# Half of the head expansion on VectorE, narrower mask matmuls and new planner constants in a two-layer attention and expert kernel

## What is computed

```python
x = x + layernorm(attn(layernorm(x)))
x = x + layernorm(ffn(layernorm(x)))
# attn: x += global causal attention; x += local attention over a window of 32 tokens
#       16 query heads of 8, 4 key/value heads, rope, norm of each q and k head, softmax
# ffn:  a shared expert plus the one expert of 8 with the highest router probability,
#       weights quantised to -1, 0, 1 times a scale for each row
```

## Time and profile before

| | us |
|---|---|
| median of 3 runs | 707.4 |
| the profiled execution, its time | 709.0 |
| the profiled execution, its span | 707.3 |
| TensorE busy | 542.5 (77%) |
| VectorE busy | 404.9 (57%) |
| ScalarE busy | 354.2 (50%) |
| GpSimd busy | 234.5 (33%) |

### The profile page before, as it was taken

One profiled execution on the slowest core, in us unless ns is written; L12 is line 12 of the kernel. 1 busy time (PEld: TensorE's weight loads), 2 busy tenths in 40 slices (PEclk: granted clock), 3 DMA queues, 4 the chain that ended last, 5 costly groups with the idle time before them and its releaser, 6 DMA issues.

```text
span 707.3 us, 15690 instructions
## 1 busy us (share of the span) xinstructions
PE 542.5 (77%) x5734; PEld 268.9 (38%) x5749; DVE 404.9 (57%) x1054; ACT 354.2 (50%) x490; POOL 234.5 (33%) x624
## 2 busy tenths in 40 slices
PE   1226649868896989889988989889999999538354
PEld 1204225424453443544444454344335343434242
DVE  2663966455476575757665566545535642654665
ACT  1021326854663578447846765666696678004010
POOL 3524784275256226411560211401110331050100
PEclk9956568997998999999999999999999999679666
DMA  8000000000000000000000000000000000000000
GB/s 233 1 0 1 1 2 1 2 1 1 2 3 1 1 10 1 2 1 9 1 2 2 8 3 1 9 2 2 9 1 2 1 10 2 1 0 2 7 0 8
DMA packets 8809, 6.17 MB, mean 9 GB/s; under 512 B 1944, under 2 KB 8096, under 8 KB 8736
## 3 DMA queue, kind: packets, MB, share of 16 engines
q10 hardware_dynamic: 3424, 2.64, 1.3%
q1 hardware_dynamic: 5312, 2.52, 1.3%
HBM read 4.11 MB, written 1.05 MB: 7 GB/s over the span
## 4 chain that ended last, share of the span: by engine, by line
PE 42%; DVE 23%; POOL 18%; issue 10%; ACT 5%; DVEq 1%; SPq 0%; DMA 0%; POOLq 0%; ACTq 0%
PE osum_g L900 11%; PE scores L874 8%; PE misc L1008 5%; ACT prob L733 5%; PE misc L997 4%; PE scores L868 3%; PE misc L900 3%; POOL qe_l L657 2%; POOL ke_l L662 2%; DVE early L1319 2%; DVE qT L1213 2%; PE misc L850 1%; PE misc L936 1%; PE misc L841 1%; DVE early L1360 1%
## 5 line engine op out<-in xcount | busy, mean ns | idle before, releaser
L733 ACT ACTIVATE prob<-scores 128x1024 f32<-128x1024 f32 (+3 forms) x352 | 307.5, 931 | 177.0 <-PE scores L874 174.2
L900 PE MATMUL osum_g<-prob,V 128*32 128x256 f32 (+1 forms) x2304 | 173.8, 392 | 12.0 <-ACT oTs_g L742 4.4
L874 PE MATMUL scores<-qT,kT 64*128 64x512 bf16 (+3 forms) x760 | 128.2, 358 | 26.9 <-ACT prob L733 13.3
L673 POOL TENSOR_SCALAR_AFFINE_SELECT prob<-prob 128x512 f32<-128x512 f32 x64 | 40.9, 660 | 140.1 <-ACT prob L733 139.9
L874 PEld LDWEIGHTS scores<-qT,kT 64*128 64x128 bf16 x760 | 34.9, 93 | 136.2 <-issue 121.9
L900 PEld LDWEIGHTS osum_g<-prob,V 128*32 128x32 f32 x2304 | 52.4, 111 | 75.8 <-issue 56.7
L1008 PE MATMUL misc<-t2T,h1p 128*128 128x512 bf16 x177 | 46.2, 414 | 10.6 <-DVE h1p L1353 5.8
L690 POOL TENSOR_SCALAR frs<-fmv 128x1 f32<-128x1 f32 x16 | 3.7, 229 | 149.6 <-DVE fmv L1376 149.4
L997 PE MATMUL misc<-early,t1T 128*128 128x256 bf16 x384 | 47.5, 285 | 1.0 <-DVEq L1322 0.6
L1360 DVE TENSOR_TENSOR early<-misc,oh 128x512 f32<-128x512 f32 x32 | 22.0, 687 | 37.3 <-PE misc L1008 36.4
L997 PEld LDWEIGHTS misc<-early,t1T 128*128 128x128 bf16 x384 | 38.2, 102 | 10.4 <-issue 3.6
(11 more groups left out here) (210 smaller groups left out, 794.1 us busy)
## 6 DMA issues: line engine op xcount, KB each, us to landing
X<-in_L_attn_hidden_dram SPq DMA_DIRECT2D x8, 128.0 KB, 4.7
early<-in_L_ffn_expert_w_dram ACTq DMA_DIRECT2D x1, 1024.0 KB, 7.6
out_dram<-X SPq DMA_DIRECT2D x16, 64.0 KB, 1.5
rope<-in_rope_dram SPq DMA_DIRECT2D x1, 256.0 KB, 3.4
early<-in_L_ffn_shared_w_dram ACTq DMA_DIRECT2D x2, 128.0 KB, 8.0
wraw_l<-in_L_attn_l_wq_dram ACTq DMA_DIRECT2D x1, 64.0 KB, 2.5
ident<-in_ident_dram SPq DMA_DIRECT2D x1, 64.0 KB, 2.4
wraw_g<-in_L_attn_g_wq_dram SPq DMA_DIRECT2D x1, 64.0 KB
```

The costliest lines, as they stand in the source:

```text
L673: pool.affine_select(out=d, in_=d, compare_op=ALU.is_ge, fill=0.0, base=0, pattern=[[0, 4], [1, P]], channel_multiplier=-1).then_inc(mask_ ...
L733: act.activation(prob[:, n % NP, :, lo:hi], src, ACT.Exp, scale=float(HD) ** -0.5).then_inc(exp_done, 1)
L874: ins = pe.matmul(o[:, :, c:c + w], kT[a][rows, g, P * (t % kept[a]):P * (t % kept[a]) + P], qT[a][rows, b % Q_KEPT[a], 2 * g:2 * g + 2, q ...
L900: ins = pe.matmul(o[32 * m:32 * m + 32, q:q + w], V[a][:, t % kept[a], g, :], prob[:, n % NP, j, c:c + w], start=(first and k == 0), stop= ...
```

## The change

The second half (i = 1) of `expand` goes from GpSimd to VectorE in all 16 fronts; each mask matmul is cut into four of 32 columns; entries of `COST`, `HOP` and `PULL` are new, and while no global score unit is left to place (`blocks` empty), the chains `local`, `attend` and `norms` have 0.5 more pull (`LATE`). The kernel's steps are otherwise the same; their order is what the planner makes of the new numbers.

```diff
+SHARED = [(a, b, 1) for a in (G, L) for b in range(NB)]
...
-    "weights": [(PE, 9.016)], "prep": [(DVE, 13.229)], "ternary": [(DVE, 3.0)], "wturn": [(PE, 0.6), (DVE, 0.6)],
-    "scales": [(DVE, 2.221), (PE, 0.428), (DVE, 1.452)], "stat": [(DVE, 0.7), (POOL, 2.0)], "norm": [(DVE, 0.7)],
+    "weights": [(PE, 9.016)], "prep": [(DVE, 13.229)], "ternary": [(DVE, 3.343)], "wturn": [(PE, 0.6), (DVE, 0.6)],
+    "scales": [(DVE, 2.406), (PE, 0.26), (DVE, 2.02)], "stat": [(DVE, 0.7), (POOL, 2.0)], "norm": [(DVE, 0.7)],
...
-    "split": [(DVE, 2.209)], "expand": [(POOL, 2.134)], "kT": [(PE, 0.8), (DVE, 0.6)], "qT": [(PE, 0.55), (DVE, 0.7)],
+    "split": [(DVE, 2.461)], "expand": [(POOL, 2.134)], "kT": [(PE, 0.8), (DVE, 0.6)], "qT": [(PE, 0.55), (DVE, 0.7)],
...
-    "oevac": [(ACT_E, 0.3)], "pv": [(PE, 0.388)], "fstat": [(DVE, 1.169), (POOL, 0.662)],
+    "oevac": [(ACT_E, 0.3)], "pv": [(PE, 0.556)], "fstat": [(DVE, 1.169), (POOL, 0.662)],
...
-    "fw1": [(PE, 3.404)], "fz": [(DVE, 0.614)], "fact": [(ACT_E, 1.229)], "fh1": [(DVE, 3.219)], "fw2": [(PE, 5.916)],
-    "fsel": [(DVE, 2.299)], "fw2s": [(PE, 0.614)], "fsum": [(DVE, 1.218), (POOL, 1.433)], "fout": [(DVE, 0.884)],
+    "fw1": [(PE, 3.404)], "fz": [(DVE, 0.534)], "fact": [(ACT_E, 1.023)], "fh1": [(DVE, 2.39)], "fw2": [(PE, 5.916)],
+    "fsel": [(DVE, 2.299)], "fw2s": [(PE, 0.768)], "fsum": [(DVE, 1.218), (POOL, 1.433)], "fout": [(DVE, 1.017)],
 }
-HOP = 0.537
+HOP = 0.803
...
+LATE = {"close": 0.0, "local": 0.5, "attend": 0.5, "norms": 0.5, "feed": 0.0}
...
 PULL = {
-    "pv": -0.5, "close": 0.66, "local": 0.9, "attend": 0.931, "norms": 1.43, "feed": 0.0, "front": 0.5, "qk": 0.0,
-    "evac": 0.3,
+    "pv": -0.5, "close": 0.806, "local": 0.9, "attend": 0.169, "norms": 0.447, "feed": 0.0, "front": 0.5, "qk": 0.0,
+    "evac": -0.073,
 }
...
+    if s[0] == "expand" and s[1:] in SHARED:
+        return [(DVE, 1.8)]
     return COST[s[0]]
...
-                options.append((tried(s, c.start())[0] - PULL[c.name], c.name, c))
+                pull = PULL[c.name] + (0.0 if blocks else LATE.get(c.name, 0.0))
+                options.append((tried(s, c.start())[0] - pull, c.name, c))
...
             def expand(a, b, i):
 
+                if (a, b, i) in SHARED:
+                    return
                 pool.wait_ge(part_ready[a], b + 1)
...
-                        pe.matmul(o[:, :, lo:end], identb[:], bias.unsqueeze(1).broadcast_to([P, 2, end - lo]),
-                                  start=True, stop=False, skip_group_check=True)
+                        for k in range(4):
+                            pe.matmul(o[32 * k:32 * k + 32, :, lo:end], identb[:, 32 * k:32 * k + 32],
+                                      bias.unsqueeze(1).broadcast_to([P, 2, end - lo]), start=True, stop=False,
+                                      skip_group_check=True)
...
+            def expand(a, b, i):
+
+                if (a, b, i) not in SHARED:
+                    return
+                dve.wait_ge(part_ready[a], b + 1)
+                if b:
+                    dve.wait_ge(kT_ready[a], b)
+                    dve.wait_ge(qT_ready[a], 2 * b)
+                for p, (lo, n) in enumerate([(0, 3), (3, 3), (6, 2)]):
+                    src = part[a][:, p, i, 0:P].rearrange("p (h d) -> p h d", d=HD)
+                    dve.tensor_copy(qe[a][:, i, :, lo:lo + n, :], src.unsqueeze(2).broadcast_to([P, H, n, HD]))
+                for p in range(3):
+                    src = part[a][:, p, i, P:QKW].rearrange("p (h d) -> p h d", d=HD)
+                    n = 3 if p < 2 else 2
+                    ins = dve.tensor_copy(ke[a][:, i, :, p::3, :], src.unsqueeze(2).broadcast_to([P, KVH, n, HD]))
+                ins.then_inc(term_ready[a], 1)
```

More of the change, by code:

```diff
@@ L115 @@
     "fohT": [(PE, 0.223), (DVE, 1.031)], "fmask": [(PE, 0.647), (DVE, 2.0)], "fw1s": [(PE, 0.624), (DVE, 0.998)],
-    "fw1": [(PE, 3.404)], "fz": [(DVE, 0.614)], "fact": [(ACT_E, 1.229)], "fh1": [(DVE, 3.219)], "fw2": [(PE, 5.916)],
-    "fsel": [(DVE, 2.299)], "fw2s": [(PE, 0.614)], "fsum": [(DVE, 1.218), (POOL, 1.433)], "fout": [(DVE, 0.884)],
+    "fw1": [(PE, 3.404)], "fz": [(DVE, 0.534)], "fact": [(ACT_E, 1.023)], "fh1": [(DVE, 2.39)], "fw2": [(PE, 5.916)],
+    "fsel": [(DVE, 2.299)], "fw2s": [(PE, 0.768)], "fsum": [(DVE, 1.218), (POOL, 1.433)], "fout": [(DVE, 1.017)],
 }
-HOP = 0.537
+HOP = 0.803
 STALL_PE, STALL_OTHER = 0.98, 0.432
-KNOBS = {"fronts": 2, "feed": 30.371}
+LATE = {"close": 0.0, "local": 0.5, "attend": 0.5, "norms": 0.5, "feed": 0.0}
+KNOBS = {
+    "fronts": 2, "feed": 30.371,
+}
 PULL = {
-    "pv": -0.5, "close": 0.66, "local": 0.9, "attend": 0.931, "norms": 1.43, "feed": 0.0, "front": 0.5, "qk": 0.0,
-    "evac": 0.3,
+    "pv": -0.5, "close": 0.806, "local": 0.9, "attend": 0.169, "norms": 0.447, "feed": 0.0, "front": 0.5, "qk": 0.0,
+    "evac": -0.073,
 }
@@ L1383, in _ @@
             run = {"weights": weights, "prep": prep, "ternary": ternary, "wturn": wturn, "scales": scales,
-                   "stat": stat, "norm": norm, "proj": proj, "split": split, "kT": k_copy, "qT": q_copy,
+                   "stat": stat, "norm": norm, "proj": proj, "split": split, "expand": expand, "kT": k_copy, "qT": q_copy,
                    "oT": o_scale, "wo": residual, "fstat": fstat, "fxa": fxa, "fh": fh_norm,
```

## The result

Twenty runs of the changed kernel took 702.98 to 706.93 us, median 704.9. Twenty of the kernel before took 706.66 to 715.32 us, median 708.8. The ratio of the two is 0.9927, 95% interval 0.9906 to 0.9947. That is some 5.2 us less (3.9 between the medians), where the forecast had 14.6.

The account below looks back on a forecast made before the run. TensorE was taken to bound the middle, GpSimd, VectorE and dependent steps the start and tail. Terms -13.2 + 2.6 - 2.0 - 2.0 = -14.6 took 709.0 to 694.4, or 693 us against the median; range 680 to 708.

Parts of the forecast that it names:

- What bounds the kernel: TensorE bounds 240 to 600 us; GpSimd and VectorE carry 60 to 106; from 600 one dependent step follows another.
- Expansion, the gain: Moving second halves off GpSimd shortens TensorE's waits for `ke` copies in all stages: 13.2 us gained.
- Start: 57 to 105 us: three second halves leave the chain (6.6 us), slower first halves give some back: 4.8 gained.
- tail: From 625.41 us to the transposes at 631.2: a half of 3.3 us covers VectorE's 1.6, 2.4 gained.
- the stretches from 180 to 600 us: Waits for `ke` copies shortened: 2.0 us gained from 180 to 240 us and 4.0 from 240 to 600.
- Expansion, VectorE's price: VectorE's copies delay its own late work: +1.6 us before the first scores, +1 (0 to 5) in the middle.
- Exclusion of the halves: Rival, chance 0.17: VectorE's and GpSimd's halves exclude each other, 3.6 us a front, 4.3 us less gain, 697 us.
- Masks: Mask tiles of 32 columns keep `pv`'s shape, saving 0.10 us behind 26 `pv`s: -2.0 us, bounds -2.6 and +11.
- weight loads that show: Worst case of the mask tiles: 29 ns for each of 6 more matmuls in 64 pairs, 11 us added.
- Order: New constants reorder every engine; local chain goes first in the tail: -2 us, bounds -15 and +20.
- the order helps more: Rival, chance 0.19: preparation leaves the first scores' way (11.8 us) or the tail's 11 us are used, 683 us.
- The slower rival: Chance 0.12: in the tail, block 6's feed is put back behind block 7's local attention, adding 16 us: 711 us.

Follow-up runs that it names:

- e2: Kernel before in its old order with whole masks, only the second half expansions moved to VectorE: 720.3 us, ratio 1.0145.
- e10: Kernel before, its order and masks, with the second half of every expansion left out from block 1 on: 700.2 us, ratio 0.9886.
- e4: Changed kernel's order with the code of the kernel before (both halves on GpSimd, whole masks): 720.6 us, ratio 1.0155 to the kernel before.
- e15: Changed kernel in its own order, VectorE's expansion copies left out from block 1 on: 700.5 us, ratio 0.9857 to the kernel before.
- e9: Kernel before and its order, VectorE additionally making the second-half copies into spare tiles nobody reads: 724.5 us, ratio 1.0228.
- e3: Kernel before in its old order, only the masks cut into tiles of 32 columns: 708.7 us, ratio 0.9991.
- e5: Changed kernel with whole masks, same new order and VectorE halves: 704.9 us, ratio 0.9928 to the kernel before.
- e1: Changed code (VectorE halves and mask tiles) under the order of the kernel before: 719.9 us, ratio 1.0147 to the kernel before.
- e6: Changed kernel with the extra pull LATE all zero, 13 places of the last block reordered: 707.5 us, ratio 0.9962 to the kernel before.
- e8: Changed kernel's new numbers and mask tiles, both halves on GpSimd and the planner told so: 701.3 us, ratio 0.9874 to the kernel before.
- e13: Repeat of e8, the same kernel: 702.1 us, ratio 0.9885 to the kernel before.
- e7: Changed code with old COST, HOP and PULL, planner told only of VectorE's 1.8 us: 734.2 us, ratio 1.0348 to the kernel before.
- e11: New COST and HOP with the old pulls, no LATE, both halves on GpSimd, mask tiles: 752.1 us, ratio 1.0633 to the kernel before.
- e12: Old COST and HOP with new PULL and LATE, both halves on GpSimd, mask tiles: 749.2 us, ratio 1.0571 to the kernel before.

## Why the forecast was right in direction and wrong in size

**What bounds the kernel:** right as a picture, but the reading of the middle misled. The earlier trace rows give VectorE 204 of 360 us, and the forecast took the rest as cover. The cover isn't spread evenly: where fronts are made VectorE runs with hardly a gap (the stretch at 281 us shown with e2).

**Expansion, the gain (13.2 us):** e10 measured 8.1. Start (forecast 4.8, measured 5.3) and tail (2.4, measured 2.9) were right. The 6.0 us of the stretches from 180 to 600 us didn't come; why not is not shown. The 8.1 holds for the old order only: in the new one the half on GpSimd (e4) costs 20 us more than a half left out (e15). And the tail's sign came true in the changed kernel without its gain: the transposes start 2.6 us behind the parts (forecast 2.5 to 3.5), but the `kT` copy stands behind `fsel` and `fsum` on VectorE and starts 6.5 us behind them, where it had been 7.0.

**Expansion, VectorE's price (2.6 us): the step that failed.** The busy times came as forecast (430 and 195, found 431 and 197), but the size of the copies by luck: 1.64 us a front was forecast, and from the first start to the last end they take 0.81 to 0.84 us in the four fronts where GpSimd makes no copies at that time and 1.04 to 1.84 in the other twelve, 1.43 on average. The forecast had one duration for both cases, and its lower bound of 1.1 was too high for the first. Their cost to the time was wrong: 16.1 us in e9, where 1.6 for the first front and 1 for the middle had been taken, with at most 5 as the bound for the middle. The middle alone cost 10. The price was bounded by the average busy share, not by the stretches in which the copies stand, and it left out that a longer wait of TensorE can be followed by a lower granted clock (0.50 instead of 1.00 in e2's stretch). That turned this part's -10.6 into +10 (e2; e9 and e10 add up to +8, the remaining 2 us are within their intervals).

**Exclusion of the halves (rival, 0.17):** the time that it gave, 697, didn't come, and the halves didn't add up to 3.6 us: both were done in 2.12. But the engines do hold each other up, and VectorE pays for it. In twelve of the 16 fronts its six copies stand beside GpSimd's and take up to 1.84 us instead of 0.84. Over the 16 fronts that is 22.9 us instead of an estimated 13.4 (16 x 0.84). The Trainium skill's page "VectorE: DVE Perf Modes" (section "Side-by-side: where the cycles go for N=2048 bf16") gives a bf16 copy in SBUF four elements a cycle in the mode with both read ports, and two in the mode with one. Two elements a cycle at that page's 0.96 GHz and some 150 cycles of fixed cost are an estimate of 356 ns for 384 elements, four of 256. The copies without GpSimd beside them took 253 to 260 ns. So this case's trace looks like the mode with both ports, the one of which the rule of the Trainium skill's page "SBUF — State Buffer" in the prediction speaks, and VectorE's copies did end only behind GpSimd's; that it is that mode was not tried separately. The mean of all copies of 384 elements, some 340 ns, is a mixture of the two cases and fits neither.

**Masks (-2.0):** the mechanism was right where a `pv` stands in front, and the sum wasn't measurable (e3, e5). The worst case, weight loads that show, didn't come. The Trainium skill's page "TensorEngine Tiling (Array Packing)", section "Key Properties", says that changing the tiling mode drains TensorE; the trace agrees, 0.10 us a change, and shows its other side, the 0.44 behind `fw2`.

**Order (-2, bounds -15 and +20): the second step that failed.** With the code in place the new order is worth -15.0 us (e1 against the changed kernel, 719.9 to 704.9), at the edge of the bound; with the old code it is worth +11 (e4). It was priced as a small term of its own, but it belongs to the code that it is made for. Of its parts only the last block's pull was priced by itself, 2.7 us (e6).

**The preparation ahead of the first scores,** the first half of the rival "the order helps more": didn't happen: the first `kT` copy starts at 50.5 us, later than before (44.3). TensorE does 4 us less in the first 60 us, and 8 more from 60 to 106. The 683 us of that rival came in no run. **The slower rival,** the last feed piling up, didn't come either: `fh` of block 7 ended 5.5 us earlier, and of block 6's feed nothing was left by then.

So the 5.2 us are the rest of large terms: some -8 us for the shorter wait and -15 for the order on one side, +16 for VectorE's queue on the other. These sizes hold for that way from the old kernel to the new one alone. Taken the other way round they are +11 for the order (e4), -20 for the shorter wait (e4 to e15, with the mask tiles) and +5 for VectorE's queue (e15 to the changed kernel). With both halves on GpSimd the same numbers make an order that gains 8 to 9 us (e8, e13). What stays open is why the planner's numbers gain only as a set; e7, e11 and e12 show that its orders lie up to 6% apart for changes of this kind, and no run isolates which steps do it.

## What to carry to other kernels

Before work is moved to an engine with a low busy share, list what that engine does in the very stretch where the work will stand, and what waits behind it; an average over a stage is no cover. Ask too whether the engine that keeps the other half will run beside it: here VectorE's copies took up to twice as long where GpSimd copied at the same time. In a kernel whose order is written out in advance, the order and the code are one change: test each alone and both together, since here +10 and +11, each alone, became -5 together. And take the wait away for nothing first (leave the step out): if that gains 8 us and the load alone costs 16, the move can't pay without another order. And where the same matmuls take twice as long in one of two traces, look at the granted clock before putting it down to a wait.

## What was not expected of the hardware

GpSimd and VectorE copied bf16 tiles from the same source at the same time, and the loss was one-sided: 2.12 us for GpSimd's six copies, 2.0 alone, but 1.77 us for VectorE's six, 0.84 alone. In the first front the second to fourth copy of VectorE each ended 0.04 to 0.11 us behind the end of a copy of GpSimd. And eight mask matmuls of 32 columns, with eight weight loads, took exactly the time of two full ones with two loads, 0.33 us for 384 columns where no change of shape came in front.
